# A chunked delta-rule scan rebuilt so that four sequences share the partitions, with its masked products multiplied out of PSUM one operation a step

## The chip, the cores and the metric

One core of a Trainium2 chip runs the whole program. The metric is the device time of one execution in microseconds (us), of which the median of three runs is given. TensorE multiplies matrices, VectorE (DVE) and ScalarE (ACT) work on rows of up to 128 partitions, GpSimd (POOL) and SyncE (SP) here set memory to zero and issue DMAs. SBUF is the working memory, PSUM holds what TensorE writes, in 8 banks of 512 f32 a partition.

## The reference, cut to what matters

Two transformer layers over 8 sequences of 512 tokens and 128 channels. The change lies in the second layer. Its attention is a delta rule over 4 heads of 32 channels, in chunks of 32 tokens, 16 chunks a sequence:

```
T = inverse(eye + strict_lower(kb @ k.T));  u = T @ v;  w = T @ kb    # for each chunk
def step(S, xs):                                                      # a scan over the chunks
    q_i, k_i, u_i, w_i = xs
    attn = where(incl_lower, q_i @ k_i.T, 0.0)
    u_adj = u_i - w_i @ S
    out_i = q_i @ S + attn @ u_adj
    S = S + k_i.T @ u_adj
```

The layer's experts are chosen from `logits = xf @ gate_W.T` over 8 experts for all 4096 tokens, by a Sinkhorn balancing that has nothing to do with the scan: 20 turns, in each of which the log-sum-exp over the experts and then that over all tokens is taken off. The two best experts of each token follow from it.

## The kernel before, in words

`program` (L2878) runs stages one after the other, with a barrier between them. Three are touched.

`project1` (L1585) makes q, k, v and beta of one sequence b at a time and stores them: normed keys and scaled keys and values as `d["tok"]` (L1638, three DMAs), channels-first q and k as `d["chan"]` (L1641), and the masked products of the chunks as `d["m"]` (L1646, 16 DMAs for each b). Its first 32 matmuls give beta, 4 columns for each tile of 128 tokens (L1711). SP issues all stores in order and, at the end, waits for them.

`filter_and_solve` (L1862) inverts the 32x32 matrices on VectorE, while TensorE does a long convolution. Its loads and its store follow the layout of `d["m"]` and `d["t"]`.

`scan` (L1952) goes over 4 tiles t of 128 tokens, and in each over 4 chunks q of 32. It carries two jobs at once, each engine's program being one hand-written order. The first is the delta rule. A tile holds one sequence's 128 tokens on the partitions and the 8 sequences side by side on the free axis, two banks of 512. `by_channel` (L2064) multiplies by the block-diagonal inverses: 32 matmuls, each of whose outputs has 32 partitions, the four heads in four different groups of 32. TensorE then makes `attn` for the whole tile (L2102) and VectorE masks it (L2266). The loop over q makes w @ S (L2113, 8 matmuls that all write the same 32 partitions, those of chunk q), q @ S (L2117, likewise), waits for VectorE's subtraction on 32 partitions (L2274), adds k.T @ u_adj to the state's banks (L2122, 8 matmuls that all read the same 32 partitions), and waits for VectorE to mask the state (L2280). After it come `attn @ u_adj` (L2131), a copy, and a transpose back (L2137).

The second job is the balancing: each of 20 turns has three round trips through TensorE, `turn_max`, `spread_max` and `sum_columns` (L2036 to L2047), between which VectorE runs `after_turn`, `after_spread` and `after_sum` (L2164 to L2192) and ScalarE two exponentials. `balance` and `balanced` put 15 such parts, five turns, between the steps of each tile. The costs come from 32 more matmuls on `gate_w` at the stage's start (L2075). After the last turn, `choose` (L2203) and `place` (L2222) give the experts and the slots.

A matmul in f32 shows as two entries each of LDWEIGHTS and MATMUL in the trace.

## Time and profile before

| what | value |
|---|---|
| runs | 2889.91, 2892.59, 2893.2 us; median 2892.59 |
| profiled execution | span 2899.3 us from first to last instruction; no other time is recorded for it |
| TensorE matmul busy | 2226.2 us, 77% of the span |
| VectorE busy | 1824.2 us, 63% |
| ScalarE busy | 1169.3 us, 40% |
| project1 | 1753 to 1926 us of the span |
| filter_and_solve | 1926 to 2064 us |
| scan | 2064.9 to 2388.3 us, 323 us |

The profile is one execution. A row of the timeline has its start, its length, the engine, the line of the kernel, the operation, what it writes and reads, how many instructions were merged into it, and in brackets the idle time before it and what ended that. Times are us from the span's start. The granted clock is a share of TensorE's full 2.4 GHz, so 0.50 is 1.2 GHz.

### The profile page before, as it was taken

The page shows a single profiled execution, that of the slowest core. Times are in us where ns is not written, and L with a number is a line of the kernel's source. Part 1 is how long each engine was busy: PE and PEld are TensorE (multiplying, and loading weights), DVE is VectorE, ACT ScalarE, POOL GpSimd, SP SyncE. Part 2 cuts the span into 40 slices and gives each one's busy share as a digit, 9 for nine tenths or more (in the row PEclk, how much of TensorE's full clock was granted, in tenths as well). Part 3 has the DMA queues.
Part 4 walks back from the last instruction along what each step waited for, and adds up shares of the span by engine and source line. Part 5 has one row for each costly group of instructions (what it writes and reads, how often), then busy time and mean ns, then how long its engine had stood idle before and what let it go on. Part 6 is the DMA issues. An engine that isn't in the chain of part 4 may idle for free. (4 is left out here: it accounts for less than half of the span.)

```text
span 2899.3 us, 44712 instructions
## 1 busy us (share of the span) xinstructions
PE 2226.2 (77%) x15735; PEld 1457.5 (50%) x15735; DVE 1824.2 (63%) x3632; ACT 1169.3 (40%) x2599; POOL 998.6 (34%) x1222
## 2 busy tenths in 40 slices
PE   5488887999999999986738326769877756759990
PEld 2244443455555555553437224438766643438880
DVE  8788876667666766664626345969366658943333
ACT  3365655556555655563203233520111115533330
POOL 4512110555555555551753670000000006753330
PEclk8699998899999999996569656865566667869995
DMA  3312121844124400000139441333522002224543
GB/s 117 98 23 45 27 41 55 205 150 164 61 89 150 138 30 1 1 1 10 51 110 284 118 102 45 102 113 108 130 45 44 23 6 50 53 71 168 182 157 92
DMA packets 216752, 251.09 MB, mean 87 GB/s; under 512 B 63062, under 2 KB 197370, under 8 KB 215194
## 3 DMA queue, kind: packets, MB, share of 16 engines
q1 hardware_dynamic: 182426, 201.68, 24.1%
q0 software_dynamic: 14432, 32.21, 3.8%
q10 hardware_dynamic: 19680, 14.42, 1.6%
q8 instruction: 124, 2.03, 0.3%
q14 instruction: 90, 0.74, 0.1%
HBM read 193.03 MB, written 125.41 MB: 110 GB/s over the span
## 5 line engine op out<-in xcount | busy, mean ns | idle before, releaser
L1005 ACT ACTIVATE a_p<-a_s_ps,a_nmax 128x512 f32<-128x512 f32 (+3 forms) x512 | 267.2, 547 | 99.1 <-DVE a_nmax L919 99.1
L919 DVE TENSOR_REDUCE a_nmax<-a_s_ps 128x2 f32<-128x1024 f32 (+3 forms) x256 | 204.8, 821 | 139.2 <-PE a_s_ps L820 134.2
L977 POOL TENSOR_SCALAR a_p<-a_p,a_rden 128x512 f32<-128x512 f32 (+3 forms) x512 | 263.8, 535 | 13.2 <-DVE a_rden L926 13.1
L597 DVE TENSOR_REDUCE a_shift<-a_s_ps 128x2 f32<-128x1024 f32 (+3 forms) x256 | 202.2, 819 | 55.6 <-PE a_s_ps L504 53.3
L1016 ACT COPY a_e<-a_pt_ps 128x1024 f32<-128x1024 f32 (+3 forms) x256 | 174.8, 714 | 111.2 <-PE a_pt_ps L833 111.2
L833 PEld LDWEIGHTS a_pt_ps<-ident,a_p 128*128 128x128 f32 x1280 | 147.4, 141 | 127.2 <-issue 67.9
L662 ACT ACTIVATE a_e<-a_s_ps 128x1024 f32<-128x1024 f32 (+1 forms) x192 | 166.0, 884 | 110.6 <-PE a_s_ps L504 110.5
L815 PE MATMUL a_s_ps<-a_kT,a_qT 64*128 64x512 f32 (+3 forms) x1024 | 191.7, 470 | 7.2 <-ACT a_p L1005 2.4
L833 PE MATMUL a_pt_ps<-ident,a_p 128*128 128x128 f32 x1280 | 173.8, 275 | 17.5 <-ACT a_e L1016 17.5
L2847 DVE TENSOR_TENSOR f_act<-f_silu,f_gu 128x256 f32<-128x256 f32 x156 | 65.7, 421 | 167.1 <-ACT f_silu L2826 166.9
L847 PE MATMUL a_y_ps<-a_e,a_v 128*64 128x512 f32 (+3 forms) x1024 | 154.3, 444 | 9.7 <-DVE acc L938 4.7
L970 POOL TENSOR_TENSOR a_qT<-a_t 128x512 f32<-128x512 f32 x64 | 81.3, 1270 | 232.3 <-DVE a_t L912 164.6
L789 PE MATMUL a_x_ps<-a_xT,a_w 128*128 128x512 f32 x256 | 148.6, 663 | 7.9 <-DMA a_xT<-xfT_d 5.5
L970 POOL TENSOR_TENSOR a_kT<-a_t 128x512 f32<-128x512 f32 x64 | 81.0, 1266 | 166.4 <-DVE a_t L912 166.4
L2725 POOL DMA_INDIRECT y_d<-f_yr,f_xr x78 | 74.9, 960 | 179.2 <-DVE f_yr L2840 167.4
L504 PE MATMUL a_s_ps<-halfb 64*128 64x128 bf16 x2048 | 124.6, 225 | 0.0
L1094 POOL DMA_INDIRECT x_d<-r_an,r_slot x96 | 95.3, 993 | 81.9 <-DVE r_slot L1162 53.0
L2826 ACT ACTIVATE f_silu<-f_gu 128x256 f32<-128x256 f32 x156 | 59.9, 384 | 154.2 <-PE f_gu L2789 153.3
L815 PEld LDWEIGHTS a_s_ps<-a_kT,a_qT 64*128 64x128 f32 x1024 | 84.7, 186 | 61.6 <-issue 43.7
L847 PEld LDWEIGHTS a_y_ps<-a_e,a_v 128*64 128x64 f32 x1024 | 69.9, 138 | 89.8 <-issue 58.4
L1005 ACT ACTIVATION_READ_ACCUMULATOR a_p<-a_s_ps,a_nmax 128x1 f32 x512 | 114.3, 223 | 0.0
L2430 POOL MEMSET g_stat<- 128x512 f32 x1 | 0.5, 525 | 318.6 <-POOLq L81 318.6
(479 smaller groups left out, 5352.9 us busy)
## 6 DMA issues: line engine op xcount, KB each, us to landing
f_w<-in_wgud SPq DMA_DIRECT2D x39, 768.0 KB, 4.4
l_band<-in_fir_long SPq DMA_DIRECT2D x16, 768.0 KB, 4.6
x_w<-in_w POOLq DMA_DIRECT2D x78, 128.5 KB, 3.8
x_xr<-x_d SPq DMA_DIRECT2D x78, 128.0 KB, 3.8
y_d<-x_yr ACTq DMA_DIRECT2D x78, 128.0 KB, 3.8
parts_d<-p_parts SPq DMA_DIRECT2D x16, 384.0 KB, 2.5
a_qs<-parts_d SPq DMA_DIRECT2D x96, 64.0 KB
a_ks<-parts_d SPq DMA_DIRECT2D x96, 64.0 KB
```

The costliest lines, as they stand in the source:

```text
L504: last = nc.tensor.matmul(out[:, h, at:at + P], st["halfb"][hh, 0, z, :], st["halfb"][hh, kind, z, :], start=False, stop=z == 1, skip_grou ...
L597: last = nc.vector.tensor_reduce(shift[n % 2][:, i, :], bank_of("q", g)[:, :, c:c + (i + 1) * P], AX.X, ALU.max, negate=True)
L662: nc.scalar.activation(e[n % 4][:, :, at:at + w], bank_of("k", g)[:, :, 0:w], ACT.Exp, scale=scale)\
L789: nc.tensor.matmul(X[:, :], w[:, k, c * P:(c + 1) * P], xT[b % 2][:, :], start=True, stop=True)\
L815: nc.tensor.matmul(out[:, h, c:c + width(i)], qT[s][hh, i * P:(i + 1) * P], kT[s][hh, 0:width(i)], start=(at == 0), stop=False, skip_group ...
L833: last = nc.tensor.transpose(pt_ps[:, h, at], p[g % 4][:, h, at], st["ident"][:, :])
L847: last = nc.tensor.matmul(Y[hh, j * P:S], v_[s][:, j, at:at + D1], e[n % 2][:, h, j, j * P:S], start=(j == 0), stop=(j == NB - 1), skip_gr ...
L919: last = nc.vector.tensor_reduce(nmax[g % 4][:, 2 * at:2 * at + 2], s_ps[g % 2][:, :, c:c + width(i)], AX.X, ALU.max, negate=True)
L970: nc.gpsimd.tensor_tensor(dst[:, :], t1[c][:, :], t2[c][:, :], ALU.add).then_inc(rot_ready, 1)
L977: last = nc.gpsimd.tensor_scalar(piece, piece, rden[g % 4][:, 2 * at + h:2 * at + h + 1], 1.0, ALU.mult, ALU.mult)
L1005: last = nc.scalar.activation(p[g % 4][:, h, c:c + width(i)], s_ps[g % 2][:, h, c:c + width(i)], ACT.Exp, bias=nmax[g % 4][:, col], accum_ ...
L1016: last = nc.scalar.copy(e[n % 2][:, :, 0:i + 1, i * P:(i + 1) * P], pt_ps[:, :, c:c + width(i)].rearrange("p h (j q) -> p h j q", q=P))
```

## The change

The diff rebuilds `scan`. Partitions now hold 32 tokens of four sequences g, and the free axis has 8 slabs e = 2q + i, chunk q of the sequences 4i + g. A step therefore touches two slabs on all 128 partitions. The matmuls of w @ S and q @ S write four groups of 32 partitions in turn, and those of k.T @ u_adj read four groups in turn. `attn` is made in each step, as products of four sequences with four, into the upper halves of the state's four banks; VectorE multiplies all of it by the mask in one 128x1024 operation, and ScalarE then sets it back to zero for the next step. The next tile's `turn_u`, `weights` and `values` stand inside the steps of the current tile, as do the output's `by_head` and `turn_back` of the tile before. Three turns of the balancing run before the first step, then one with each step. The result is moved to its place by 16 SBUF-to-SBUF DMAs a tile. The costs' matmuls move to `project1`, as 8 more columns of those for beta. `d["tok"]`, `d["m"]` and `d["t"]` change their layout, with 12 stores instead of 3 and 4 instead of 16 for each b in `project1`. The work of the convolution and of the solve stays.

The core of the diff (indented less; removed lines of `scan` stand in the print above):

```
+            for c in range(NB):
+                cc = slice(c * CH, (c + 1) * CH)
+                sp.dma_start(d["tok"][i, :, b % NB, :, c, b // NB, :].rearrange("t s e -> s t e"), src[cc, :, :])\
+                    .then_inc(tok_stored[z], 16)
...
+        for c in range(NB):
+            cc = slice(c * CH, (c + 1) * CH)
+            sp.dma_start(d["m"][b % NB, c, b // NB, :, :, :, :].rearrange("h t i j -> i (h t) j"),
+                         m[z][cc, :, :, cc].rearrange("i h t j -> i (h t) j")).then_inc(m_stored[z], 16)
...
+        last = nc.tensor.matmul(beta_ps[:, n * per_tile:(n + 1) * per_tile], st["hsT"][:, tile(n)],
+                                w[:, 3 * P:3 * P + per_tile], start=True, stop=True)
     last.then_inc(beta_done, 1)
...
+    nc.scalar.activation(beta[:, :, :].rearrange("p b (t h) -> p b t h", h=HL), logits[:, :, :, 0:HL], ACT.Sigmoid)\
         .then_inc(beta_ready, 1)
+    nc.scalar.mul(st["cost"][:, :, :].rearrange("p (b t) e -> p b t e", b=B), logits[:, :, :, HL:per_tile],
+                  float(-1.0 / SK_EPS)).then_inc(cost_ready, 1)
     a.wait_ge(zero, 1)
...
+    def load_uw(t):
+        after(sp, w_done, 2 * t)
+        for i, dst in ((2, vb), (1, kb)):
+            sp.dma_start(dst[:, :, :], d["tok"][i, t, :, :, :, :, :].rearrange("g s q i c -> (g s) (q i) c"))\
+                .then_inc(uw_in, 16)
+        sp.wait_ge(zero, 1)
+        for g in range(NB):
+            sp.dma_start(inv[lanes[g], :, lanes[g]], d["t"][g, :, :, :, t, :, :].rearrange("q i h m j -> m (q i h) j"))\
+                .then_inc(uw_in, 16)
+
+    def load_qk(t):
+        after(sp, at_done, NB * t)
+        after(sp, rd_done, NB * t)
+        sp.dma_start(qT[:, :, :], d["chan"][0, :, :, t * P:(t + 1) * P].rearrange("b c s -> c b s")).then_inc(qk_in, 16)
+        for q in range(NB):
+            sp.dma_start(kT[:, q, :, :], d["chan"][1, :, :, t * P + q * CH:t * P + (q + 1) * CH].rearrange("b c s -> c b s"))\
+                .then_inc(qk_in, 16)
+
+    def move_out(t):
+        sp.wait_ge(added, 2 * t + 2)
+        for g in range(NB):
+            for q in range(NB):
+                sp.dma_start(delta[lanes[q], :, g, t, :], outs[t % 2][lanes[g], 2 * q:2 * q + 2, :]).then_inc(moved, 16)
+
+    load_uw(0)
...
     for t in range(NB):
...
+        if t + 1 < NB:
+            load_uw(t + 1)
+            load_qk(t + 1)
+        move_out(t)
+    sp.wait_ge(moved, 16 * NB * NB * NB)
...
+    def load_kn(t):
+        after(gp, ds_done, NB * t)
+        gp.dma_start(kn[:, :, :], d["tok"][0, t, :, :, :, :, :].rearrange("g s q i c -> (g s) (q i) c")).then_inc(kn_in, 16)
+
+    nc.gpsimd.memset(inv[:, :, :], 0.0).then_inc(zero, 1)
...
+    for t in range(NB):
+        load_kn(t)
...
+    def project(t, q):
+        after(pe, state_ready, t * NB + q)
+        if q == 0:
+            pe.wait_ge(w_ready, 2 * t + 2)
+        for i in range(2):
+            for g, gg in enumerate(lanes):
+                last = nc.tensor.matmul(ws_ps[gg, i * P:(i + 1) * P], wT[t % 2][:, 2 * q + i, gg],
+                                        state_[:, four * i + g, :], start=True, stop=True)
...
+    def attend(t, q):
+        after(pe, at_clear, t * NB + q)
+        for i in range(2):
+            some = slice(four * i, four * i + four)
+            for h, hh in enumerate(lanes):
+                last = nc.tensor.matmul(at_ps[:, h, i * P:(i + 1) * P], kT[hh, q, some, :], qT[hh, some, lanes[q]],
+                                        start=False, stop=False, skip_group_check=True)
+        last.then_inc(at_done, 1)
+
+    def update(t, q):
+        pe.wait_ge(ua_ready, t * NB + q + 1)
+        if q == 0:
+            pe.wait_ge(kn_in, 16 * (t + 1))
+        for i in range(2):
+            for g, gg in enumerate(lanes):
+                last = nc.tensor.matmul(DS[:, g, i * P:(i + 1) * P], kn[gg, 2 * q + i, :], ua[gg, 2 * q + i, :],
+                                        start=False, stop=False, skip_group_check=True)
+        last.then_inc(ds_done, 1)
...
+        pe.wait_ge(ua_ready, (t + 1) * NB)
+        pe.wait_ge(at_ready, (t + 1) * NB)
+        if s == 1:
...
+            pe.wait_ge(added, 2 * t)
...
+    turn_max(0)
+    spread_max(0)
+    sum_columns(0)
+    pe.wait_ge(zero, 2)
+    for g in range(NB):
+        clear(DS[:, g, :])
+    turn_max(1)
+    turn_u(0, 0)
+    turn_u(0, 1)
+    spread_max(1)
+    weights(0, 0)
+    sum_columns(1)
+    weights(0, 1)
+    turn_max(2)
+    project(0, 0)
+    values(0, 0)
+    values(0, 1)
+    spread_max(2)
+    read(0, 0)
+    attend(0, 0)
+    sum_columns(2)
+    update(0, 0)
+    for t in range(NB):
+        more = t + 1 < NB
+        if t:
+            turn_max(turn(t, 0))
+            by_head(t - 1, 1)
+            spread_max(turn(t, 0))
+            read(t, 0)
+            sum_columns(turn(t, 0))
+            attend(t, 0)
+            update(t, 0)
+            turn_back(t - 1, 0)
+        for q in range(1, NB):
+            i = turn(t, q)
+            if i < SINKHORN:
+                turn_max(i)
+            if q == 1 and t:
+                turn_back(t - 1, 1)
+            elif q == 2 and more:
+                turn_u(t + 1, 1)
+            elif q == 3 and more:
+                weights(t + 1, 1)
+            if i < SINKHORN:
+                spread_max(i)
+            project(t, q)
+            if i < SINKHORN:
+                sum_columns(i)
+            read(t, q)
+            attend(t, q)
+            if more or q + 1 < NB:
+                update(t, q)
+            if more:
+                (turn_u, weights, values)[q - 1](t + 1, 0)
+        if more:
+            i = turn(t, NB)
             turn_max(i)
+            values(t + 1, 1)
             spread_max(i)
...
+            project(t + 1, 0)
             sum_columns(i)
...
+        v.wait_ge(ws_done, t * NB + q + 1)
+        v.wait_ge(u_ready, 2 * t + 2)
+        after(v, outT_done, 2 * t)
+        pair = lambda ap: ap[:, 2 * q:2 * q + 2, :]
+        nc.vector.tensor_tensor(pair(ua), pair(u[t % 2]), ws_ps[:, 0:2 * P].rearrange("p (i c) -> p i c", i=2),
+                                ALU.subtract).then_inc(ua_ready, 1)
+
+    def advance(t, q):
+        v.wait_ge(ds_done, t * NB + q + 1)
+        nc.vector.tensor_tensor(state_[:, :, :].rearrange("p (i g) c -> p g i c", i=2),
+                                DS[:, :, 0:2 * P].rearrange("p g (i c) -> p g i c", i=2),
+                                bc(bc(hmask[:, :], 2), four), ALU.mult).then_inc(state_ready, 1)
+
+    def masked(t, q):
+        v.wait_ge(at_done, t * NB + q + 1)
+        after(v, outT_done, 2 * t)
+        nc.vector.tensor_tensor(at[:, :, 2 * q:2 * q + 2, :], at_ps.rearrange("p h (i c) -> p h i c", i=2),
+                                bc(bc(mask[:, :], 2), HL), ALU.mult).then_inc(at_ready, 1)
+
+    def add_out(t, s):
+        some = slice(four * s, four * s + four)
+        v.wait_ge(back_done, 2 * t + s + 1)
+        v.wait_ge(rd_ready, (t + 1) * NB)
+        nc.vector.tensor_tensor(outs[t % 2][:, some, :], outs[t % 2][:, some, :],
+                                bank(t, s, NB - 1)[:, :].rearrange("p (e c) -> p e c", c=P), ALU.add).then_inc(added, 1)

...
+    for i in range(TURNS_FIRST):
+        after_turn(i)
+        after_spread(i)
+        after_exps(i)
+        if i == TURNS_FIRST - 1:
+            v.wait_ge(consts_in, 32)
+            adjust(0, 0)
+        after_sum(i)
+    for t in range(NB):
+        if t:
+            i = turn(t, 0)
+            after_turn(i)
+            after_spread(i)
+            after_exps(i)
+            adjust(t, 0)
+            after_sum(i)
+            add_out(t - 1, 0)
+        for q in range(1, NB):
+            i = turn(t, q)
+            if i < SINKHORN:
+                after_turn(i)
+            advance(t, q - 1)
+            if q == 1 and t:
+                add_out(t - 1, 1)
+            if i < SINKHORN:
+                after_spread(i)
+                after_exps(i)
+            adjust(t, q)
+            masked(t, q - 1)
+            if i < SINKHORN:
+                after_sum(i)
+        if t + 1 < NB:
+            i = turn(t, NB)
+            after_turn(i)
+            advance(t, NB - 1)
+            after_spread(i)
+            after_exps(i)
+            masked(t, NB - 1)
+            after_sum(i)
+    masked(NB - 1, NB - 1)
+    v.wait_ge(gate_in, 48)
     step(nc.vector.tensor_copy(below_b[:, :], below[:, :]))
...
     choose()
+    add_out(NB - 1, 0)
+    add_out(NB - 1, 1)
     place()
...
+    def clear_at(t, q):
+        a.wait_ge(at_ready, t * NB + q + 1)
+        nc.scalar.copy(at_ps.rearrange("p h (i c) -> p h i c", i=2),
+                       blank[:, :].unsqueeze(1).unsqueeze(1).to_broadcast([P, HL, 2, P])).then_inc(at_clear, 1)
+
...
+    def logs(i):
+        if i < SINKHORN and i % FOLD == FOLD - 1:
+            a.wait_ge(sums_ready, i // FOLD + 1)
+            nc.scalar.activation(rlog[:, :], rlog[:, :], ACT.Ln)
+            nc.scalar.activation(clog[:, :], clog[:, :], ACT.Ln).then_inc(logs_ready, 1)
...
+        for q in range(1, NB):
+            i = turn(t, q)
+            if i < SINKHORN:
+                row_exps(i)
+            if q == 2 and more:
+                copy_uT(t + 1, 1)
+            elif q == 3 and more:
+                copy_w(t + 1, 1)
+            if i < SINKHORN:
+                column_exps(i)
+            clear_at(t, q - 1)
+            copy_rd(t, q)
+            logs(i)
+            if more:
+                (copy_uT, copy_w, copy_u)[q - 1](t + 1, 0)
+        if more:
+            i = turn(t, NB)
+            row_exps(i)
+            copy_u(t + 1, 1)
+            column_exps(i)
+            clear_at(t, NB - 1)
+            logs(i)
+            copy_outT(t, 0)
+    copy_outT(NB - 1, 0)
+    copy_outT(NB - 1, 1)
```

## Rows read from the trace of the kernel before

**Rows 1.** Windows: length, busy PE, PEld, DVE, ACT, POOL, granted clock, DMA share, GB/s.

```profile
2153.00:2225.00 72.00, 55.96 (x507) 45.92 (x499) 44.37 (x108) 12.43 (x25) 0.00 (x0) 0.69 0.20 45
2082.00:2083.00 1.00, 1.00 (x10) 0.23 (x12) 0.93 (x3) 0.00 (x0) 0.00 (x0) 0.50 1.16 290
2086.00:2092.00 6.00, 5.33 (x116) 4.33 (x109) 2.35 (x7) 3.46 (x7) 0.00 (x0) 1.00 0.52 80
```

**Rows 2.** Timeline, one step of the scan (tile 0, chunk 2), PE and DVE.

```profile
2120.77 3.62 PE L2113 MATMUL c_ps<-c_state,c_wT 128*32 128x128 f32 x16 [1.38 <-DVE c_state L2280]
...
2124.18 3.19 PE L2117 MATMUL c_ps<-c_state,c_qT 128*32 128x128 f32 x16
...
2124.43 1.29 DVE L2274 TENSOR_TENSOR c_ua<-c_u,c_ps 32x512 f32<-32x512 f32 x2 [1.63 <-PE c_ps L2113]
...
2127.62 2.05 PE L2122 MATMUL c_ps<-c_ua,c_kn 32*128 32x128 f32 x16
...
2130.41 1.28 DVE L2280 TENSOR_TENSOR c_state<-c_ps,c_hmask 128x512 f32<-128x512 f32 x2
```

**Rows 3.** Timeline, groups whose matmuls use different 32-partition groups, and one small group.

```profile
2082.75 3.43 PE L2069 MATMUL c_ps<-c_inv,c_vb 128*32 128x128 f32 x64
...
2086.32 1.96 PE L2069 MATMUL c_ps<-c_inv,c_kb 128*32 128x128 f32 x64
...
2090.46 1.16 PE L2102 MATMUL c_ps<-c_qT,c_kT 32*128 32x128 f32 x28 [0.41 <-ACT c_u L2319]
...
2091.88 0.39 PE L2047 MATMUL c_ps<-k_cpart,k_ones 128*128 128x8 f32 x2 [0.26 <-DVE k_cpart L2179]
```

**Rows 4.** Groups by line and form: count, busy us, mean ns, idle before.

```profile
L1116 DVE TENSOR_TENSOR acc<-acc,r_an 128x1024 f32<-128x1024 f32 x4 | 4.9, 1225 | 0.1
...
L1016 ACT COPY a_e<-a_pt_ps 128x1024 f32<-128x1024 f32 x64 | 64.8, 1012 | 109.1 <-PE a_pt_ps L833 109.1
...
L2266 DVE TENSOR_TENSOR s<-c_ps,c_mask 128x512 f32<-128x512 f32 x32 | 19.8, 681 | 0.0
```

**Rows 5.** Timeline, VectorE's parts of one balancing turn, and its wait for the logarithms.

```profile
2141.63 0.15 DVE L2183 COPY k_csum<-c_ps 128x8 f32<-128x8 f32 x1
...
2143.76 0.61 DVE L2162 TENSOR_REDUCE k_cm<-k_zc 128x8 f32<-128x256 f32 x1
...
2145.90 0.27 DVE L2171 TENSOR_SCALAR k_topb<-k_one,k_top 8x128 f32<-8x128 f32 x1
...
2148.25 0.17 DVE L2175 COPY k_cmb<-c_ps 128x8 f32<-128x8 f32 x1 [2.08 <-PE c_ps L2042]
...
2149.86 0.62 DVE L2179 TENSOR_REDUCE k_cpart<-k_ez 128x8 f32<-128x256 f32 x1
...
2153.94 0.17 DVE L2189 TENSOR_TENSOR k_cmb<-k_cmb,k_clog 128x8 f32<-128x8 f32 x1 [1.93 <-ACT k_clog L2350]
```

**Rows 6.** Timeline, the start of the scan stage.

```profile
2064.90 0.17 DVE L2248 MEMSET k_ones<- 128x128 f32 x1 [30.55 <-PEq L81]
...
2068.04 13.82 PE L2075 MATMUL c_ps<-k_w,hsT 128*128 128x8 f32 x64 [4.46 <-DMA k_tiles<-in_tiles]
```

**Rows 7.** SP's DMA issues in the timeline, and one row of issues (KB, us to landing).

```profile
1916.72 7.59 SPq L1646 DMA_DIRECT2D m_d<-q_m  x16
...
2076.80 3.00 SPq L2026 DMA_DIRECT2D c_kn<-tok_d  x1
...
2159.97 2.31 SPq L2018 DMA_DIRECT2D c_inv<-t_d  x4
...
c_inv<-t_d SPq DMA_DIRECT2D x16, 128.0 KB, 3.5
```

**Rows 8.** Timeline, the end of the scan stage and the first DMA of the next.

```profile
2369.33 0.42 DVE L2204 TENSOR_TENSOR k_z<-k_zc,k_rlog 128x256 f32<-128x256 f32 x1
...
2381.23 0.17 DVE L2226 TENSOR_SCALAR k_need<-c_ps 128x8 f32<-128x8 f32 x1 [4.03 <-PE c_ps L2145]
...
2388.30 0.83 SPq L2419 DMA_DIRECT2D g_w<-in_mlp  x2
```

More of the change, by code:

```diff
@@ L2047, in sum_columns, with clear, by_channel @@
                 nc.tensor.matmul(k_ps[:, 0:NE2], ones[:, :], cpart[:, :], start=True, stop=True).then_inc(csum_done, 1)
-            def balance(t, n):
-                i, part = t * FOLD + n // 3, n % 3
-                if part == 0:
+            def clear(bank):
+                nc.tensor.matmul(bank, zeros[0:1, 0:P], zeros[0:1, :], start=True, stop=False, skip_group_check=True)
+            def by_channel(to, src, s, rhs):
+                for e in range(four * s, four * s + four):
+                    for h, hh in enumerate(lanes):
+                        last = nc.tensor.matmul(to[hh, e % four * P:(e % four + 1) * P], src[:, e, hh], rhs(e, h),
+                                                start=True, stop=True)
+                return last
@@ L2343, in _ @@
+            copy_w(0, 1)
+            row_exps(2)
+            copy_u(0, 0)
+            copy_u(0, 1)
+            column_exps(2)
+            copy_rd(0, 0)
+            for t in range(NB):
+                more = t + 1 < NB
+                if t:
+                    i = turn(t, 0)
                     row_exps(i)
[L2344 to L2345 removed]
+                    copy_outT(t - 1, 1)
                     column_exps(i)
[L2347 removed]
```

382 lines of the change are left out of this document (149 added, 233 removed).

## The prediction

> **What bounds the kernel now.** I read three views. The windows give each stage's share of each engine: in a tile of the scan, 72 us, TensorE is busy 56.0 and VectorE 44.4 us, at a granted clock of 0.69, between the two levels of 1.2 and 2.4 GHz [rows 1]. The timeline of one step then shows which wait ends last [rows 2]. The reader should follow one circle in it: eight matmuls of w @ S (16 entries) last 3.62 us, VectorE's subtraction ends 1.33 after them, but TensorE takes up the state's products only after q @ S, 3.19 us; those last 2.05, then VectorE masks the state, 1.28, and the next step may begin. From 2120.77 to 2131.69 that is 10.9 us, of which TensorE holds 8.9. Third, the same view shows groups whose matmuls go to different groups of 32 partitions: 64 entries of the same shape as w @ S last 3.43 or 1.96 us, against 3.62 for 16 [rows 3]. The long one began at a clock of 0.50, the short one ran at 1.00 [rows 1]. So the scan is bound by TensorE's serial small groups, and the same matmuls spread over four partition groups cost a quarter or less.
>
> **What the change leaves on TensorE.** w @ S and q @ S become 16 entries each over four groups: from [rows 3] 0.05 us an entry at the slow and 0.03 at the fast clock, with some 0.2 of latency 0.7 to 1.0 us each. Attend and update are spread over four input groups like the row of 28 entries in 1.16 us: 0.75 for one, 1.4 for both in a row. A half of `by_channel` costs 1.0 to 1.7, I take 1.35; a half of `values` no more. TensorE then has some 7 us of work in a step, so VectorE's list sets the pace.
>
> **VectorE's list.** A balancing turn has three parts [rows 5]: sum to column maxima 2.74 (2141.63 to 2144.37), on to the top 1.80 (to 2146.17), column part with its exponential 2.23 (2148.25 to 2150.48), in all 6.77. The scan adds for each step advance and masked, 1.23 each as for 128x1024 [rows 4], and adjust on 128x256, 0.42 like the row at 2369.33 [rows 8]. The masked products gain nothing by themselves: eight operations of 0.62 a tile become four of 1.23. The gain in VectorE's own time is the subtraction, 1.29 to 0.42 a step. The new additions cost 0.68 twice a tile. The logarithms cost 2.5 once a tile (1.93 of waiting and three small operations [rows 5]).
>
> **Where it stalls.** ScalarE runs in order: clear, copies, then the next row exponential. Counted from the end of adjust: masked to 1.23, clear (1.01 for 128x1024 [rows 4]) to 2.3, attend and update to 3.7, the next tile's half group to 5.05, ScalarE's copy (estimate 0.6, a little over half of the 1.01 for twice the width) to 5.65, exponential to 6.15. VectorE is ready at 1.23 + 2.74 = 3.97. It waits 2.2 us, after chunks 1 and 3 of tiles 0 to 2; after chunk 2 the logarithms cover it. This is also what is late next once TensorE is relieved.
> Second, SP's list puts the 16 copies of `move_out(t)` ahead of `load_uw(t+2)`, and `turn_u(t+2, 0)` on TensorE waits for those loads, with the copy, the exponential and so VectorE behind it. No row shows an SBUF-to-SBUF copy. Sixteen stores from 32 partitions took 7.59 us to issue; the dearest single issue took 3.00 [rows 7]. I take the former as the nearest in shape: 0.47 each. From the last addition: copies to 7.6, two loads 1.2 (at the 0.58 of the inverse ones) and four inverse loads 2.3, landing 3.5 [rows 7], so 14.6; then half group, copy, exponential: 17.0. VectorE is ready at 2.23 + 0.42 + 3.97 = 6.6. That is 10.4 us, 8.2 more than the 2.2 already counted, in tiles 1 and 2. The load for tile 1 has no copies ahead of it.
>
> **The sum for the scan.**
> - Start: memsets 1.3 (estimate, six at the 0.17 of the first and its gaps [rows 6]), maxima 2.35, first turn 1.80 + 2.23 + 2.74 and two round trips of 0.5 (0.39 of matmul [rows 3] and hops), second turn 9.7 with a whole slow `turn_u`, third to adjust 6.05: 27.2. The 13.82 us of cost matmuls that began at 2068.04 [rows 6] are gone from here; the memset of the inverses on POOL (nothing waits behind it but SP's loads) and those loads land inside the first turns.
> - Tile 0: first step 2.74 + 1.80 + 1.23 + 2.23 + 0.42 = 8.42; second 9.65 + 2.2; third 9.65 + 2.5; then the turn without adjust 11.43, and the turn into the next tile 9.22, where a round trip stands bare (0.8). Together 53.1.
> - Tiles 1 and 2: + 1.4 of additions + 8.2: 62.7 each. Tile 3 has only two turns left and no loads: 9.8, 9.65 and 11.0, 30.4.
> - End: choose to place took 11.9 and place to the next stage 7.07 [rows 8]; the cast of `below` 0.3, ScalarE's last exponential behind two copies and two half groups of the output 2.8, the last 16 copies beyond place 1.0. Together 23.1.
> Sum 259.2 us. The stage now lasts from 2064.90 to 2388.30 [rows 6, 8], 323.4. So 64.2 are saved.
>
> **The other stages.** `project1`: the last 16 stores take 7.59 us [rows 7]; four take about 2.3, the price of the four inverse loads, and land at most 2 us later than the small ones (128 KB took 3.5). I take 4.0 saved, bounds 2 and 5.5. Twelve token stores instead of three lie in the middle of each b; at 0.47 they are 5.6 us, and the 12 m stores that go give as much back. Eight more columns for beta: 64 entries by 8 columns at the slow clock, 0.5 (nothing to 0.9). Kn's load moves to POOL's queue, where only the previous kn is ahead; it has more than a step until update. The q and k loads, of which k becomes four of shorter pieces, have some 13 us until `read`, against 2.8 of issuing and 3.5 to land.
> In all 64.2 + 4.0 - 0.5 = 67.7 on the execution of 2899.3 us, whose span lies 0.2% above the median. The spread around a span isn't shown, so I take the same difference off the median: 2892.6 - 67.7 = 2825.
>
> **Two rules against the sum.** Within a step TensorE changes between groups of 128x32, 32x128 and full matmuls five or six times. In the rows, the small group at 2091.88 started 0.26 us after its engine went idle, when its input came, so a change shows no price above a hop [rows 3]. The Trainium skill, TensorEngine Tiling (Array Packing), section Tiling Modes, says that changing the tiling mode drains TensorE. By it, with an estimate of 0.3 us for each of the two changes in each of the 6 stalled chains, the time would be 2829.
> The clock was 0.69 with TensorE busy 78% of a tile [rows 1], and it will be less busy. At 1.2 GHz throughout, half groups cost 1.7, attend and update 2.0: 0.9 us in each of 6 stalls, and some 4 at the start and the end, 2834. The Trainium skill, TensorE: Matmul & The Clock Gate, last section (on what matters for kernels), says that idle gaps bring the lower clock; the sum above goes by a middle value.
>
> **The rivals.**
> A, the loads don't stall: copies issue at a fraction of 0.47, or the inverses land early. For it: they are asynchronous and small. Against it: every issue in [rows 7] cost 0.47 or more. 2825 - 16 = 2809, with the fast clock on top, the mirror of the slow one, 2800.
> B, the coupled queues cost more: slow clock (+ 9), and 1.0 us an issue, between the rows: + 0.53 x 16 in two tiles and at the end, + 25: 2859. For it: four engines wait for one another in every turn, and my chain counts one hop at each place.
> C, the four partition groups don't run side by side when the input changes with each matmul. Per step w @ S and q @ S cost 3.6 and 3.2 again, attend and update 2.05 each; in the chains they add 5.2 us nine times and 3.5 seven times: 71 us, 2896, no change. That is also the case in which the change doesn't do what it says. [rows 3] speaks against it: there, too, each matmul has its own input.
> D, slower: SP. Each `move_out` holds SP so long that the next loads come late, in tiles 1 and 2 and at the end: 48 x (p - 0.47) on top. It decides from p = 2.0 us; at 3.0, the dearest issue [rows 7], the time is 2825 + 121 = 2946. Against it: that issue came at the end of the stage's first burst of loads, and these copies are 32 KB each and have no burst ahead of them.
>
> **How the numbers follow.** Forecast 2825: 0.5. A 0.15, B 0.24, C 0.04, D 0.07. The range takes A at the fast clock and B with issues somewhat dearer than 1.0: 2798 to 2872. About 0.2% is what a measurement here can tell from no change. Faster by more than that: forecast, A and B, with the small share of D below 2 us: 0.9. Same: C, 0.03. Slower: D, 0.07.
>
> **What would show it.** Right: entries of w @ S in groups of 16 lasting 0.7 to 1.0 us; VectorE's idle time small inside a step but for two waits on ScalarE's row exponential a tile; SP's list with 16 issues of about 0.47 ahead of the inverse loads, and `turn_u(t+2, 0)` waiting on those; a scan of 250 to 270 us. Wrong: groups of 16 at 3 us (C), issues over 1 us (B, D), TensorE never waiting on the inverse loads (A), or a saving outside the scan above 5 us.

## The result, and the profile after

| | before | after |
|---|---|---|
| median (range) | 2892.2 us (2889.9 to 2893.2) | 2849.7 us (2846.9 to 2857.7) |
| ratio, 95% interval | | 0.9854 (0.9837 to 0.9871) |
| span of the profiled execution | 2899.3 us | 2856.1 us |
| `project1`, from its first load to the next stage's load of `d["m"]` | 173.1 us | 168.9 us |
| scan, first memset to the next stage | 323.4 us | 281.4 us |

Faster by 42.5 us in the medians and 43.2 in the two profiled executions; of these the scan has 42.0 and `project1` 4.2. The rest grew by 3; the rows here don't show where. The forecast was 67.7 faster, 2825; 2849.7 lies inside the range of 2798 to 2872.

First the engines over two stretches of the scan (columns: stretch, its us, busy us and instructions of PE, PEld, DVE, ACT and POOL, granted clock, DMA share, GB/s).

```profile
2085.00:2145.00 60.00, 40.12 (x507) 29.05 (x506) 41.27 (x101) 18.70 (x34) 0.56 (x1) 0.53 0.24 47
2220.00:2280.00 60.00, 31.42 (x400) 22.66 (x404) 33.49 (x79) 14.98 (x26) 0.53 (x1) 0.51 0.27 62
```

TensorE went from 78% busy at a clock of 0.69 [rows 1] to 67 and 52% at 0.53 and 0.51, the lower level of 1.2 GHz nearly throughout these two stretches; over the scan from 2065 to 2320 the granted clock is 0.56. Now chunk 1 of tile 0, TensorE's side of the timeline:

```profile
2096.04 1.08 PE L2137 MATMUL c_ws_ps<-c_state,c_wT 128*32 128x128 f32 x16 [0.54 <-DVE c_state L2322]
2098.13 0.59 PE L2093 MATMUL c_k_ps<-k_cpart,k_ones 128*128 128x8 f32 x2 [1.00 <-DVE k_cpart L2297]
2098.65 1.08 PE L2148 MATMUL c_rd_ps<-c_state,c_qT 128*32 128x128 f32 x16
2100.64 1.24 PE L2157 MATMUL c_ds_ps<-c_qT,c_kT 32*128 32x128 f32 x16 [0.91 <-ACT c_ds_ps L2450]
2101.65 1.08 PE L2167 MATMUL c_ds_ps<-c_ua,c_kn 32*128 32x128 f32 x16
2102.66 1.94 PE L2103 MATMUL c_bulk_ps<-c_inv,c_vb 128*32 128x128 f32 x32
```

The 3.62, 3.19 and 2.05 us of [rows 2] have become 1.08 each. Each of the last two rows starts 1.01 after the one above, though the first of these two steps keeps the shape (32x128) and the second changes it to 128x32. The same stretch on ScalarE and VectorE:

```profile
2104.66 0.58 ACT L2462 COPY c_turned<-c_bulk_ps 128x512 f32<-128x512 f32 x1 [3.77 <-PE c_bulk_ps L2103]
2105.14 0.42 ACT L2442 ACTIVATE k_ez<-k_z 128x256 f32<-128x256 f32 x1
2105.59 0.43 DVE L2282 TENSOR_TENSOR k_ez<-k_ez,k_crec 128x256 f32<-128x256 f32 x1 [3.39 <-ACT k_ez L2442]
2110.62 0.41 DVE L2317 TENSOR_TENSOR c_ua<-c_u,c_ws_ps 128x256 f32<-128x256 f32 x1
2110.95 1.22 DVE L2329 TENSOR_TENSOR s<-c_ds_ps,c_mask 128x1024 f32<-128x1024 f32 x1
```

VectorE waits 3.39 us for an exponential that stands in ScalarE's list behind the copy of the next tile's half group. In tile 1 the same wait looks like this, with SP's list ahead of it:

```profile
2153.43 10.41 SPq L2051 DMA_DIRECT2D three<-c_outs  x16
2163.89 0.58 SPq L2032 DMA_DIRECT2D c_vb<-tok_d  x1
2164.51 0.44 SPq L2032 DMA_DIRECT2D c_kb<-tok_d  x1
2164.99 4.60 SPq L2036 DMA_DIRECT2D c_inv<-t_d  x4
2172.81 1.93 PE L2103 MATMUL c_bulk_ps<-c_inv,c_vb 128*32 128x128 f32 x32 [12.66 <-DMA c_inv<-t_d]
2175.74 0.42 DVE L2282 TENSOR_TENSOR k_ez<-k_ez,k_crec 128x256 f32<-128x256 f32 x1 [16.11 <-ACT k_ez L2442]
```

The 16 copies, which wait for VectorE's last addition of the output, hold SP for 10.4 us, the inverse loads follow, and VectorE stands for 16.1. The end of the scan, in order of time:

```profile
2316.32 1.94 PE L2103 MATMUL c_bulk_ps<-s,c_ua 128*32 128x128 f32 x32 [1.39 <-issue]
2319.04 1.94 PE L2103 MATMUL c_bulk_ps<-s,c_ua 128*32 128x128 f32 x32 [0.79 <-ACT c_turned L2477]
2321.64 1.28 ACT L2533 ACT_TABLE_LOAD   x1
2323.38 0.29 DVE L2343 TENSOR_SCALAR c_u<-k_z 128x256 f32<-128x256 f32 x1 [6.11 <-ACT k_ez L2533]
2331.18 10.19 SPq L2051 DMA_DIRECT2D three<-c_outs  x16
2339.49 0.17 DVE L2381 CAST owner<-k_owner 1x39 int32<-1x39 f32 x1
2343.76 0.52 POOL L2611 MEMSET g_stat<- 128x512 f32 x1 [74.36 <-POOLq L81]
```

VectorE waits 6.11 for the last exponential, and SP's issuing of the copies ends 1.7 us after VectorE's last operation (2339.66); the next stage begins 2.4 us behind it, so that the copies, not VectorE, let it start.

### The profile page after: what moved, and what is told of

It reads as the page before. It is cut to its first block and busy times, and to the rows that moved or that the text cites. A ratio compares the mean times of both kernels' runs of the same rounds, so it can differ in the third digit from the quotient of the medians.

```text
span 2856.1 us, 44572 instructions
## 1 busy us (share of the span) xinstructions
PE 2142.5 (75%) x15617; PEld 1374.8 (48%) x15617; DVE 1809.4 (63%) x3589; ACT 1186.3 (42%) x2623; POOL 998.2 (35%) x1227
## 3 DMA queue, kind: packets, MB, share of 16 engines
q1 hardware_dynamic: 188170, 201.69, 24.7%
```

## Experiments

All are edits of the changed kernel. The scan begins at times that differ by some 12 us between single executions, so each run is read by its **scan stretch**: from VectorE's first operation on the costs to the first memset of the next stage. A stretch is that of one execution. e4, whose edit turned out to do nothing, lies 0.1 from after; how far two executions of one kernel differ isn't shown otherwise. The ratio goes by the kernel before as timed beside that run, with medians of 2892.2 to 2896.2.

| kernel | median us | ratio to before (95%) | scan stretch us | against after |
|---|---|---|---|---|
| after | 2849.7 | 0.9854 (0.9837 to 0.9871) | 280.4 | |
| e1_loads_first | 2822.0 | 0.9756 (0.9731 to 0.978) | 256.0 | -24.4 |
| e6_moves_on_pool | 2826.9 | 0.977 (0.9753 to 0.9786) | 257.6 | -22.8 |
| e2_row_exp_first | 2843.3 | 0.9822 (0.9805 to 0.9838) | 276.0 | -4.4 |
| e3_last_exp_first | 2842.0 | 0.9814 (0.9795 to 0.9833) | 275.9 | -4.5 |
| e4_by_group | 2851.2 | 0.9847 (0.983 to 0.9864) | 280.3 | -0.1 |
| e5_one_group | 2853.1 | 0.986 (0.9838 to 0.9881) | 284.7 | +4.3 |
| e11_all_one_group | 2889.7 | 0.9978 (0.9967 to 0.9989) | 318.3 | +37.9 |
| e10_masked_in_four | 2852.3 | 0.9855 (0.9834 to 0.9876) | 282.8 | +2.4 |
| e9_masked_on_pool | 2844.1 | 0.9832 (0.9808 to 0.9855) | 277.4 | -3.0 |
| e7_all_three | 2795.0 | 0.9661 (0.9641 to 0.9681) | 226.8 | -53.6 |
| e8_split_end | 2796.5 | 0.9661 (0.9642 to 0.9679) | 223.5 | -56.9 |
| e12_with_masks_moved | 2807.6 | 0.9694 (0.9676 to 0.9711) | 238.9 | -41.5 |

### What the waits cost: SP's order

```diff
             for t in range(NB):
+                if t == 0:
+                    load_uw(1)
                 if t + 1 < NB:
-                    load_uw(t + 1)
                     load_qk(t + 1)
+                if t + 2 < NB:
+                    load_uw(t + 2)
                 move_out(t)
```

> Only SP's list changes: the loads of u, w and the inverses for tile t+2 are issued ahead of the 16 output copies of tile t, not behind them. Theory (the copies hold the loads back): the 16.1 us that VectorE waits at the row exponential after chunk 1 of tiles 1 and 2 shrink to the 3.4 us of tile 0, where no copies are ahead; 2 x 12.7 = 25 us saved, 2849.7 - 25 = 2824, and TensorE no longer waits on the inverse loads. Rival 1 (the wait would be there anyway, because ScalarE and TensorE come late in these chunks): less than 8 us saved, 2842 or more. Rival 2 (what is moved back becomes late: the q and k loads or the copies that free the output buffer): the two long waits vanish but a new one of over 5 us stands at q @ S or at ScalarE's copy of it, time 2830 to 2845.

Measured: -24.4 us. Of the waits, listed as the waiting and the awaited instruction, us in total, times and longest, these rows are of after:

```profile
DVE k_ez L2282 <- ACT k_ez L2442: 49.1, 12, 16.1
PE c_bulk_ps L2103 <- DMA c_inv<-t_d: 25.1, 2, 12.7
```

and this one is of e1, where TensorE has no wait on the inverse loads left:

```profile
DVE k_ez L2285 <- ACT k_ez L2445: 24.2, 12, 3.4
```

49.1 - 24.2 is 24.9, the whole gain. The second way to the same end moves `move_out` to GpSimd's queue:

```diff
-                        sp.dma_start(delta[lanes[q], :, g, t, :], outs[t % 2][lanes[g], 2 * q:2 * q + 2, :]).then_inc(moved, 16)
+                        gp.dma_start(delta[lanes[q], :, g, t, :], outs[t % 2][lanes[g], 2 * q:2 * q + 2, :]).then_inc(moved, 16)
```

> The 16 output copies of each tile are issued by GpSimd's queue, which holds only the four loads of kn, in place of SP's. Theory (SP's order alone makes the long wait): as with the loads put first, the two waits of 16 us fall to 3.4, 25 to 28 us saved, 2822 to 2825, less what the last 16 copies cost more or less than SP's 10.2 us at the end. Rival (the copies are slower from GpSimd, 1 us each or more): the waits fall as well, but the end of the scan is 6 us or more later, 2831 or above.

Measured: -22.8. VectorE's waits at the row exponential fall to 23.8, as in e1. GpSimd's queue issues the 16 copies in 8.4 us, faster than SP's 10.2, but the end of the scan is later all the same:

```profile
2298.06 8.44 POOL L2071 DMA_DIRECT2D three<-c_outs  x16 [30.13 <-DVE c_outs L2340]
2314.46 0.53 POOL L2615 MEMSET g_stat<- 128x512 f32 x1 [7.97 <-POOLq L81]
```

From the start of the last copies to the next stage it is 16.4 us here and 12.6 in after, 3.8 more, where the rival had named 6 or more. Its reason, the issuing, is not it: the time lies behind the last issue (8.0 us, against 2.4), and no run shows what it is.

Both runs take the long wait away, one by moving the loads and one by moving the copies, so it was the place of the copies ahead of the loads on SP's list.

### What the waits cost: ScalarE's and TensorE's order

In e2, after `logs(i)`, ScalarE does `row_exps(i + 1)` and only then the next tile's copy; TensorE does `turn_max(i + 1)` ahead of the next tile's half group.

```diff
                     logs(i)
+                    if i + 1 < SINKHORN and (more or q + 1 < NB):
+                        row_exps(i + 1)
                     if more:
                         (copy_uT, copy_w, copy_u)[q - 1](t + 1, 0)
```

> ScalarE does the next turn's row exponential ahead of its copy for the next tile, and TensorE the transpose of the column maxima ahead of the next tile's half group; SP's list is as in the changed kernel. Theory (VectorE stands behind the next tile's group and copy in ScalarE's order): in tile 0 the waits of 3.4, 1.8 and 2.5 us go (the one behind the logarithms down to the table load, about 0.5); in tiles 1 and 2 the first is limited by the late loads and gives about 1, the others as in tile 0. In all 7 + 5 + 5 = 17 us, 2833. Rival (the halves are then late themselves, and TensorE's later groups take up what was won): under 6 us saved, 2844 or more, with TensorE's project or spread of the maximum late after its half group.

Measured: -4.4, not -17. VectorE in the chunk that was shown above for after:

```profile
2090.49 0.42 DVE L2283 TENSOR_TENSOR k_ez<-k_ez,k_crec 128x256 f32<-128x256 f32 x1
2095.49 0.17 DVE L2292 COPY k_cmb<-c_k_ps 128x8 f32<-128x8 f32 x1 [1.99 <-PE c_k_ps L2088]
```

The wait of 3.39 at the exponential is gone and one of 1.99 stands at the spread of the maximum: TensorE does that behind the second half group, which waits for ScalarE's copy of the first. After the logarithms it is 2.66, and in tiles 1 and 2 the wait for the late loads stands there too (15.6 at the longest). The rival was right, and it names the place.

For the end of the scan, the last exponential ahead of the two copies:

```diff
-            copy_outT(NB - 1, 0)
-            copy_outT(NB - 1, 1)
             a.wait_ge(last_ready, 1)
             nc.scalar.activation(ez[:, :, :], z[:, :, :], ACT.Exp).then_inc(last_exp, 1)
+            copy_outT(NB - 1, 0)
+            copy_outT(NB - 1, 1)
```

> At the end of the scan ScalarE does the last exponential ahead of its two copies of the output. Theory: VectorE's wait of 6.1 us in the choice of experts falls to about 1.9 (table load 1.28, exponential 0.42, hops), and the 16 output copies on SP, which end the stage, begin 4.2 us earlier: 2849.7 - 4.2 = 2845.5. Rival (the output additions wait for the copies that are now later, so SP's tail stays): the wait falls, but the stage ends no more than 1.5 us earlier, 2848.

Measured: -4.5. The wait fell further than expected, to 0.48, since the table load now runs ahead of it:

```profile
2309.74 1.28 ACT L2531 ACT_TABLE_LOAD   x1
2313.09 0.42 ACT L2531 ACTIVATE k_ez<-k_z 128x256 f32<-128x256 f32 x1 [2.07 <-DVE k_z L2341]
2313.54 0.29 DVE L2343 TENSOR_SCALAR c_u<-k_z 128x256 f32<-128x256 f32 x1 [0.48 <-ACT k_ez L2531]
```

e7 has all of these, and what e2 had shown to be missing: TensorE's second half group behind `spread_max` and `project`, its copy behind the column exponential.

```diff
-                    elif q == 2 and more:
-                        turn_u(t + 1, 1)
-                    elif q == 3 and more:
-                        weights(t + 1, 1)
                     if i < SINKHORN:
                         spread_max(i)
                     project(t, q)
+                    if q == 2 and more:
+                        turn_u(t + 1, 1)
+                    elif q == 3 and more:
+                        weights(t + 1, 1)
```

> The loads ahead of the copies, the row exponential and the transpose ahead of the next tile's first half group, the second half group and its copy behind the spread of the maximum and the column exponential, and the last exponential ahead of the output copies. Theory (the waits are separate places of one chain and add up): 28 for the loads, 2 x 3.4 + 2 x 2.5 + 1.8 for each kind of wait in tiles 0 to 2, about 20 together, 6 at the end: 2849.7 - 54 = 2796. Rival (each is only the latest of several waits that lie close behind one another): half of the 20 is left, 2806 or more, with TensorE's groups as VectorE's releasers.

Measured: -53.6 where 54 were expected; of this 24.4 (e1) are the loads, for which 28 were expected, 4.5 (e3) the end, for which 6 were, and the rest the order within the steps. Between 2083.38 and 2125.97 the only idle times of VectorE are the column exponentials' 0.48 and one at the logarithms:

```profile
2090.08 0.43 DVE L2300 TENSOR_TENSOR k_ez<-k_ez,k_rrec 128x256 f32<-128x256 f32 x1 [0.48 <-ACT k_ez L2450]
2099.41 0.42 DVE L2300 TENSOR_TENSOR k_ez<-k_ez,k_rrec 128x256 f32<-128x256 f32 x1 [0.48 <-ACT k_ez L2450]
2104.97 0.17 DVE L2311 TENSOR_TENSOR k_cmb<-k_cmb,k_clog 128x8 f32<-128x8 f32 x1 [2.42 <-ACT k_clog L2487]
```

Less e1's 24.4 and e3's 4.5, the order within the steps is worth 24.7, about the 24.2 that VectorE still waited at the row exponential in e1. The granted clock is higher as well, 0.65 over the scan against 0.56, and no run separates what shorter groups on TensorE gave. e8 adds a split of the last 16 copies:

```diff
-                for g in range(NB):
+                for g in range(NB if t + 1 < NB else NB // 2):
...
+            a.wait_ge(added, 2 * NB)
+            for g in range(NB // 2, NB):
+                for q in range(NB):
+                    nc.scalar.dma_start(delta[lanes[q], :, g, NB - 1, :],
+                                        outs[(NB - 1) % 2][lanes[g], 2 * q:2 * q + 2, :]).then_inc(moved, 16)
```

> The kernel with all three reorderings, and of the last tile's 16 output copies eight are issued by ScalarE's queue, idle by then. Theory (SP's 16 issues of 0.64 us end the scan, some 2.8 us behind VectorE's placing): SP ends 5.1 us earlier, the placing becomes the end, 3 us saved on that kernel, 2792. Rival (the landing or the shared DMA engines, not the issuing, set the end): no gain, 2795.

Measured: 3.3 us off the stretch, as expected; the medians, 2795.0 and 2796.5 on two chips, don't show it. VectorE's last operation and the next stage's first:

```profile
2273.27 0.17 DVE L2385 CAST owner<-k_owner 1x39 int32<-1x39 f32 x1
2274.62 0.52 POOL L2622 MEMSET g_stat<- 128x512 f32 x1 [63.45 <-POOLq L81]
```

### What the partition groups are worth

```diff
-                for i in range(2):
-                    for g, gg in enumerate(lanes):
+                for g, gg in enumerate(lanes):
+                    for i in range(2):
                         last = nc.tensor.matmul(ws_ps[gg, i * P:(i + 1) * P], wT[t % 2][:, 2 * q + i, gg],
```

and the same for `rd_ps`.

> In w @ S and q @ S the two matmuls of one partition group follow each other, in place of a round over the four groups; the results are the same. Theory (the groups overlap because neighbours in the order go to different partitions): 16 entries take about five steps of 0.45 in place of two, 2.2 us and not 1.08, for each of the 32 groups; of this some 0.3 to 0.6 us a step reach VectorE's path, 5 to 10 us, 2855 to 2860. Rival (TensorE looks further ahead, or the order doesn't matter): the entries stay at 1.1 us and the time at 2849.7 within 2.

Measured: nothing, and the groups last as long. In chunk 2 of tile 0:

```profile
2099.68 1.10 PE L2137 MATMUL c_ws_ps<-c_state,c_wT 128*32 128x128 f32 x16 [0.75 <-DVE c_state L2322]
```

The rival was right: two matmuls of one group behind each other don't hold up the next groups. Is it the groups at all? e5 writes them all to the first one:

```diff
-    last = nc.tensor.matmul(ws_ps[gg, i * P:(i + 1) * P],
+    last = nc.tensor.matmul(ws_ps[gg if t + q == 0 else lanes[0], (i * P if t + q == 0 else g * P):(i * P if t + q == 0 else g * P) + P],
                             wT[t % 2][:, 2 * q + i, gg], state_[:, four * i + g, :], start=True, stop=True)
```

and the same for `rd_ps`.

> All matmuls of w @ S and q @ S after the first step write the same 32 partitions, in the same number, shape and order; their products are put over one another, so the output is left wrong. Every other instruction and wait is that of the changed kernel. Theory (the four partition groups run side by side, and that is what the change gives): 16 entries last 3.4 to 3.6 us and not 1.08, as in the kernel before; w @ S adds 1.7 us to a step, and where the next tile's half group follows it adds 3.4, about 9 x 3.4 + 7 x 1.7 = 43 us, 2893. Rival (as the last run's order of the groups suggests, the entries are quick for another reason, such as their inputs, and one group is as quick as four): entries near 1.1 us, 2849.7 within 3.

The first half of the theory holds, the second falls. TensorE in the same chunk:

```profile
2102.72 3.27 PE L2137 MATMUL c_ws_ps<-c_state,c_wT 128*32 128x128 f32 x16 [0.75 <-DVE c_state L2322]
2106.23 1.93 PE L2148 MATMUL c_rd_ps<-c_state,c_qT 128*32 128x128 f32 x16
2108.68 0.73 PE L2157 MATMUL c_ds_ps<-c_qT,c_kT 32*128 32x128 f32 x16 [0.51 <-ACT c_ds_ps L2450]
2109.23 0.62 PE L2167 MATMUL c_ds_ps<-c_ua,c_kn 32*128 32x128 f32 x16
2109.78 1.08 PE L2103 MATMUL c_bulk_ps<-c_inv,c_kb 128*32 128x128 f32 x32
```

One group of partitions makes 3.27 of 1.08 (3.62 in the chunk before this one), and yet the stretch grows by 4.3 us only. VectorE's waits show why:

```profile
DVE c_ua L2317 <- PE c_ws_ps L2137: 16.2, 11, 3.7
DVE k_ez L2282 <- ACT k_ez L2442: 36.7, 7, 15.6
```

The longer w @ S does cost VectorE time, 16.2 us of waiting where after has 1.2. But the wait at the row exponential falls from 49.1 to 36.7 and gives 12.4 back. Two things can pay for that: q @ S ends before what is behind it may start (the row of L2157 still waits 0.51 for ScalarE's clear), and the granted clock rose from 0.56 to 0.75 over the scan (2065 to 2320), so that the groups left as they were last 0.73, 0.62 and 1.08 in place of 1.24, 1.08 and 1.94. No run separates the two. e11 takes the spread from the keys' products and the update too:

```diff
-    last = nc.tensor.matmul(at_ps[:, h, i * P:(i + 1) * P], kT[hh, q, some, :], qT[hh, some, lanes[q]],
+    last = nc.tensor.matmul(at_ps[:, h, i * P:(i + 1) * P], kT[lanes[0], q, some, :], qT[lanes[0], some, lanes[q]],
...
-    last = nc.tensor.matmul(DS[:, g, i * P:(i + 1) * P], kn[gg, 2 * q + i, :], ua[gg, 2 * q + i, :],
+    last = nc.tensor.matmul(DS[:, g, i * P:(i + 1) * P], kn[lanes[0], 2 * q + i, :], ua[lanes[0], 2 * q + i, :],
```

> As with one group of partitions for w @ S and q @ S, and now also the keys' products and the state's update read 32 partitions only, so that none of the four runs side by side; the output is left wrong (each sequence group's part is taken from the first, and the products lie over one another). Theory (TensorE had room for the first two kinds beside VectorE's list, and for these it has not: per step 2.7 us more, of which about 1 reaches an ordinary chain and all of it the three with a half group): 7 x 1 + 9 x 2.7 = 31 us above the run before, 2875 to 2885. Rival 1 (my case C, all of it on the path): 2896. Rival 2 (the granted clock rises to near 1.00 and hides it): 2853 to 2860.

Measured: +37.9, of which 33.6 come from these two, near the 31 of the theory; the median of 2889.7 lies above its 2875 to 2885. The clock was 0.73, as in e5, so rival 2 falls. A step is long again:

```profile
2105.39 3.42 PE L2137 MATMUL c_ws_ps<-c_state,c_wT 128*32 128x128 f32 x16 [0.75 <-DVE c_state L2322]
2109.06 1.94 PE L2148 MATMUL c_rd_ps<-c_state,c_qT 128*32 128x128 f32 x16
2111.50 2.05 PE L2157 MATMUL c_ds_ps<-c_qT,c_kT 32*128 32x128 f32 x16 [0.51 <-ACT c_ds_ps L2450]
2113.39 1.95 PE L2167 MATMUL c_ds_ps<-c_ua,c_kn 32*128 32x128 f32 x16
```

Without the four groups side by side the change is worth 6 us of the 42 (2896.2 before in the same comparison, 2889.7): the spread is the gain. The two kinds that stand between adjust and the next half group last 2.65 us a step longer than in e5, 42 us in 16 steps, and 33.6 of them reach the time. That they cost so much because the first two kinds had used up TensorE's slack is an argument; no run has these two alone.

### What the masked products are worth

```diff
-                nc.vector.tensor_tensor(at[:, :, 2 * q:2 * q + 2, :], at_ps.rearrange("p h (i c) -> p h i c", i=2),
-                                        bc(bc(mask[:, :], 2), HL), ALU.mult).then_inc(at_ready, 1)
+                for h in range(HL):
+                    last = nc.vector.tensor_tensor(at[:, h, 2 * q:2 * q + 2, :], at_ps[:, h, :].rearrange("p (i c) -> p i c", i=2),
+                                                   bc(mask[:, :], 2), ALU.mult)
+                last.then_inc(at_ready, 1)
```

> The changed kernel with each masked product as four operations of 128x256, one for a head, in place of one of 128x1024. Theory (one operation a step is worth only the fixed part of an instruction): four take 0.35 to 0.42 us each, 1.4 to 1.7 in place of 1.22, 16 x 0.2 to 0.5 on VectorE's path, 3 to 7 us, 2853 to 2857. Rival (other waits cover it): 2849.7 within 2.

Measured: +2.4, from one execution of each, between the theory's 3 to 7 and the rival's 2; the operations agree with it, 1.41 us for four against 1.22, 16 x 0.19 = 3.0:

```profile
2086.43 1.41 DVE L2330 TENSOR_TENSOR s<-c_ds_ps,c_mask 128x256 f32<-128x256 f32 x4
```

Then not on VectorE at all:

```diff
             def clear_at(t, q):
-                a.wait_ge(at_ready, t * NB + q + 1)
+                a.wait_ge(at_done, t * NB + q + 1)
...
+                nc.scalar.copy(at[:, :, 2 * q:2 * q + 2, :], at_ps.rearrange("p h (i c) -> p h i c", i=2)).then_inc(at_copied, 1)
+                a.wait_ge(at_copied, t * NB + q + 1)
...
+            def masked(t, q):
+                gp.wait_ge(at_copied, t * NB + q + 1)
+                some = at[:, :, 2 * q:2 * q + 2, :]
+                nc.gpsimd.tensor_tensor(some, some, bc(bc(mask[:, :], 2), HL), ALU.mult).then_inc(at_ready, 1)
```

> VectorE no longer multiplies the masked products out of PSUM: ScalarE copies them to SBUF (one more 128x1024 operation, 1.0 us a step) and GpSimd, idle until then, multiplies them there. Theory (VectorE's list sets the pace of a step, and the masked product is 1.22 us of it): 16 x 1.22 = 19.5 us saved, 2830, with the waits on ScalarE as they were. Rival 1 (ScalarE's list becomes the pace in its turn): under 8 us saved, 2842 or more. Rival 2 (GpSimd's multiplication slows VectorE at the SBUF port they share): VectorE's operations of 0.42 us last longer beside it, 2845 or more.

Measured: -3.0 of the 19.5. Rival 2's mechanism is in the trace: VectorE's `k_z<-cost,k_cmb` has a mean of 0.90 us for 0.42, 20 x 0.48 = 9.6, and its four copies of the row sums take 1.14 each for 0.18, 3.8 more. Rival 1's is there too: the last exponential is waited for 9.8 us and not 6.1. Do the long waits of tiles 1 and 2 hide a gain besides? In e12 they are gone:

> All three reorderings, the split end, and the masked products by ScalarE's copy and GpSimd's multiplication. Theory (with the waits gone VectorE's list is the whole pace, so that taking 1.22 us out of each step now pays in full): 16 x 1.22 = 19.5 us below the kernel with the split end, 2772. Rival 1 (GpSimd's 2.35 us beside it lengthens some of VectorE's operations by about 1 us, as one copy of 0.18 us lasted 1.14 in the run before): 4 to 10 us gained, 2782 to 2788. Rival 2 (ScalarE's list is too long): waits on ScalarE's exponentials of over 0.5 us stand in each step, nothing gained.

Measured: 15.4 us **worse** than e8, although 16 operations of 1.22 have left VectorE. Neither the theory nor a rival had a loss: rival 1 named the mechanism at a fraction of its price, and rival 2's waits stand in three steps, not in each. What took their place, in time order on GpSimd and VectorE:

```profile
2170.65 2.35 POOL L2084 TENSOR_TENSOR s<-s,c_mask 128x1024 f32<-128x1024 f32 x1 [10.61 <-ACT s L2459]
2170.71 2.58 DVE L2291 TENSOR_TENSOR k_z<-k_z,k_rm 128x256 f32<-128x256 f32 x1
```

An operation of 0.42 us that starts 0.06 behind GpSimd's ends 0.29 behind it. VectorE's rows of this line have a mean of 1.03, and those of L2289 0.62, against 0.42 in e8: 20 x 0.61 + 20 x 0.20 = 16 us of the 19.5. All ten operations of these two lines that overlap a multiplication end 0.27 to 0.29 behind it. Beside another multiplication, the first two VectorE rows keep their time:

```profile
2091.97 2.35 POOL L2084 TENSOR_TENSOR s<-s,c_mask 128x1024 f32<-128x1024 f32 x1 [30.72 <-ACT s L2459]
2092.71 0.17 DVE L2316 COPY k_csum<-c_k_ps 128x8 f32<-128x8 f32 x1 [0.36 <-PE c_k_ps L2107]
2092.91 0.20 DVE L2317 RECIPROCAL k_crec<-k_csum 128x8 f32<-128x8 f32 x1
2093.15 1.46 DVE L2289 TENSOR_TENSOR k_z<-cost,k_cmb 128x256 f32<-128x256 f32 x1
```

The two stretched lines read two tensors in SBUF. Of the short rows the copy reads one, in PSUM, and the reciprocal one, in SBUF; the subtraction, which reads one in each, keeps its 0.41 as well (at 2091.94). New waits of 6.3 us at the column sum, 4.2 at the row exponential, 1.9 at the logarithms, 2.3 at the last exponential and 1.1 at the counts of `place` come on top, and 2.9 more lie in a cast and a copy held up in the same way. Less the 19.5 and a wait of 2.4 that go, that makes 12.8 of the 15.4; the rest these rows don't show. The Trainium skill, GPSIMD Engine Reference, in the table of the engine's specifications, says that GpSimd's SBUF interfaces are shared with VectorE, with contention where a VectorE instruction has two SBUF inputs or runs in a mode with two ports. This trace agrees on the two-input rows; why the cast and the copy are held and the reciprocal isn't, no run here tells apart.

## Why the prediction was right in direction and 25 us short

It was right that the circle through TensorE's small groups was the bound, that spreading them is what pays (e11), and that SP's copies ahead of the loads are late next (e1, e6). It was wrong in the sizes of the waits, all in one direction, and 2849.7 lies in the range only since that reaches to case B. Of its signs of being right, 16 entries of w @ S in 0.7 to 1.0 us (1.08), issues of 0.47 (0.65) and a scan of 250 to 270 us (281.4) were missed. The sum for the scan was 259.2 us, and 281.4 were measured:

| part | forecast | measured |
|---|---|---|
| start, to the end of adjust(0,0) | 27.2 | 27.5 |
| tile 0 | 53.1 | 56.0 |
| tile 1 | 62.7 | 69.8 |
| tile 2 | 62.7 | 69.3 |
| tile 3 | 30.4 | 31.3 |
| end | 23.1 | 27.5 |

- **SP's issue time was the term that failed most.** "I take the former as the nearest in shape: 0.47 each", and 0.58 for each inverse load. Measured: 10.41 / 16 = 0.65 and 4.60 / 4 = 1.15. The chain from the last addition to the landing was 14.6; it took 19.4 (2153.41 to 2172.81), 4.8 more in each of two tiles, 9.6 of the 22.2 us by which the sum is short. That is case B's mechanism at a third of its price for a copy, 0.18 above the 0.47 and not 0.53, with slower inverse loads that B didn't have. e1 and e6 show that what the two waits have above 3.4 us hangs on it; case A gave 16 us for its absence, and it was 24.4.
- **The copies on ScalarE.** Waits of 2.2 after chunks 1 and 3 were 3.4 and 2.5. "After chunk 2 the logarithms cover it" was wrong: 1.8 of waiting, because the exponential behind them needs its table loaded again (1.28 at 2117.89), after the copy. About 3 us a tile.
- **The clock.** "The sum above goes by a middle value"; it was 0.56 over the scan. Half groups cost 1.94, not the 1.35 taken, and attend with update 2.0, not 1.4: together the 1.2 us by which the chunk-1 wait was missed. The prediction's own sum for the lower level, 2834, was nearer. The Trainium skill, TensorE: Matmul & The Clock Gate, section Why this matters for your kernels, says that idle gaps bring the lower clock. The trace agrees: with TensorE busy 58% of 2065 to 2320, in place of 75% of the scan before, the granted clock was 0.56 and not 0.67.
- **Changes of shape on TensorE** have no price in the rows of chunk 1: 1.01 us from group to group with a change and without. The Trainium skill, TensorEngine Tiling (Array Packing), section Tiling Modes, says that changing the tiling mode drains TensorE; the 2829 that the prediction set beside it isn't borne out.
- **The end.** "ScalarE's last exponential behind two copies and two half groups of the output 2.8": VectorE waited 6.11, with the table load and half groups of 1.94. And the 16 copies (10.2) let the next stage begin 3.0 us later behind the start of `place` than in the kernel before; 1.0 had been allowed. Together 4.4 over.
- **Case C** (no overlap, + 71) was excluded by [rows 3], rightly. Made by hand it costs 37.9. My price put w @ S and q @ S on the path in full: they cost 4.3. That C's 2896 is near e11's 2889.7 is luck, a price 33 us too high on a sum 25 too low.
- **The masked products** "gain nothing by themselves": one operation instead of four in a step is worth 2.4 to 3 us; no run sets it against the eight of 128x512 a tile of the kernel before. Taking them off VectorE gave 3.0 us in e9 and lost 15.4 in e12.
- `project1` saved 4.2 (forecast 3.5), and the start and tile 3 held within 1 us. So did VectorE's prices: 1.22 and 1.20 for the 1.23, 0.41 for the 0.42.

The kernel with the reorderings (e7, e8) beats both: 0.966 of the time before, 98 and 100 us, against the change's 42.

## What to carry to other kernels

When a change relieves the engine that was the bound, its gain is decided by the order of the lists on the other queues: here some 57 further us of the scan lay in which of two things SP, ScalarE and TensorE did first, and in who issued the last copies. Put what the next chain waits for ahead of what only frees a buffer, on every queue of that chain at once: moving the exponential and one transpose alone gave 4 us, and all three kinds of reordering together left VectorE's list as the pace. How the 25 us within the steps divide isn't shown, since no run has e2's two moves with the loads first. And before an operation goes to an idle engine, look whether the two engines can run beside each other on these operands.

## What the chip showed that was not expected

- Making two of TensorE's groups 2 to 3 times as long cost 4.3 us in the scan; the granted clock rose from 0.56 to 0.75, and the other groups were shorter (0.73, 0.62 and 1.08 us for 1.24, 1.08 and 1.94).
- Of w @ S and q @ S, taking the four partition groups in turn or two matmuls of each at a time made no difference (1.08 and 1.10 us); one group in place of four did (3.27 and 3.62).
- Four loads of 128 KB took SP 2.17 us to issue at the start of the scan, 2.7 us behind the last issue, and 4.56 to 6.07 later, directly behind other issues (after and e1). The issue time of the same four loads isn't fixed; what sets it no run separates.
- An operation of VectorE with two SBUF inputs that started beside GpSimd's multiplication lasted until 0.3 us behind its end, ten times out of ten in e12 (2.58 us for 0.42 at the longest).
